# Down weights of a mixture-of-experts stage split in two counted halves, and a small copy moved from VectorE to ScalarE

## The reference

```
xe = zeros(E, CAP, d).at[se, pos].set(xf[tok])      # E = 64 experts, CAP = 256 slots each, d = 512
h  = silu(xe @ gate_proj) * (xe @ up_proj)          # 512 -> 192
ye = h @ down_proj                                  # 192 -> 512
out[tok] += ye[se, pos] * weight                    # added to the rows the tokens came from
```

## Time and profile before

| | |
|---|---|
| Median of three runs | 1779.56 us (1773.2 to 1784.63) |
| The profiled execution | 1779.15 us, with a span of 1777.3 us |
| Attention part | 0 to about 1183 us |
| Expert stage | about 1183 us to the end, about 594 us |
| Loads of one expert, time from issue to landing (median, whole run) | rows 4.6 us, gate/up 6.4 us, down 7.3 us |
| Bytes moved in the whole run | 311.91 MB |

### The profile page before, as it was taken

One profiled execution on the slowest core, in us unless ns is written; L12 is line 12 of the kernel. 1 busy time (PEld: TensorE's weight loads), 2 busy tenths in 40 slices (PEclk: granted clock), 3 DMA queues, 4 the chain that ended last, 5 costly groups with the idle time before them and its releaser, 6 DMA issues.

```text
span 1777.3 us, 25068 instructions
## 1 busy us (share of the span) xinstructions
PE 1576.7 (89%) x8112; PEld 1012.7 (57%) x8112; DVE 1211.1 (68%) x2706; ACT 982.4 (55%) x1922; POOL 956.0 (54%) x890
## 2 busy tenths in 40 slices
PE   5888899999999999999999989529999999999995
PEld 2444344544544444444444543229988888888884
DVE  3566587787787787787788776317876666665762
ACT  3345457656656656656665745215555555555552
POOL 4122243474464464464465456756676666665665
PEclk8889999999999999999999989759999999999997
DMA  9956743634544444343343240059999999999995
GB/s 333 293 166 205 222 137 109 190 129 153 171 143 152 143 145 135 116 123 114 101 114 96 57 109 23 25 184 252 258 241 253 256 262 252 255 262 256 244 253 84
DMA packets 148337, 311.91 MB, mean 175 GB/s; under 512 B 27674, under 2 KB 37786, under 8 KB 148208
## 3 DMA queue, kind: packets, MB, share of 16 engines
q1 hardware_dynamic: 109296, 238.89, 43.3%
q0 software_dynamic: 38912, 71.43, 18.1%
HBM read 141.25 MB, written 155.91 MB: 167 GB/s over the span
## 4 chain that ended last, share of the span: by engine, by line
PE 36%; DMA 22%; issue 10%; DVE 9%; POOL 5%; SPq 2%; ACT 1%; POOLq 0%; DVEq 0%; ACTq 0%
DMA out_rows<-y_slots,row_ids 18%; PE bank L686 6%; PE bank L698 5%; PE bank L677 4%; DMA q_stack<-x_t 2%; PE bank L616 2%; POOL slot_rows L1460 2%; PE bank L655 2%; SPq L440 2%; PE bank L720 2%; POOL out_rows L1509 1%; PE bank L609 1%; PE bank L642 1%; PE bank L595 1%; DVE row_stat L1073 1%
## 5 line engine op out<-in xcount | busy, mean ns | idle before, releaser
L1198 DVE TENSOR_REDUCE max_col<-bank 128x1 f32<-128x512 f32 x512 | 340.7, 684 | 148.5 <-PE bank L677 147.4
L953 ACT ACTIVATE p_t<-bank 128x512 f32<-128x512 f32 x512 | 297.9, 596 | 256.7 <-PE bank L686 252.0
L1448 POOL TENSOR_TENSOR p_sum<-p_t 128x512 f32<-128x512 f32 x128 | 162.1, 1282 | 330.6 <-ACT p_t L953 329.9
L1509 POOL DMA_INDIRECT out_rows<-y_slots,row_ids x128 | 221.8, 1733 | 197.4 <-DMA out_rows<-y_slots,row_ids 150.1
L1460 POOL DMA_INDIRECT slot_rows<-row,slot_i x256 | 268.1, 1047 | 78.2 <-issue 77.6
L686 PE MATMUL bank<-q_stack,k_stack 98*128 98x512 f32 x512 | 277.6, 543 | 15.1 <-DMA q_stack<-max_lo 14.5
L677 PE MATMUL bank<-k_stack,q_stack 96*128 96x512 f32 x512 | 213.4, 418 | 24.7 <-DVE max_col L1198 14.5
L686 PEld LDWEIGHTS bank<-q_stack,k_stack 98*128 98x128 f32 x512 | 98.5, 193 | 193.3 <-issue 176.1
L1499 POOL TENSOR_TENSOR down_lo<-down,down_hi 96x1024 fp32r<-96x1024 f32 x64 | 188.5, 2945 | 15.9 <-DVE down_hi L1356 15.9
L1325 DVE TENSOR_TENSOR x_slots_t_lo<-bank,x_slots_t_hi 128x512 fp32r<-128x512 f32 x128 | 88.3, 690 | 150.6 <-ACT x_slots_t_hi L1005 150.6
L795 PE MATMUL bank<-gate_up_hi,x_slots_t_hi 128*128 128x384 f32 x512 | 185.2, 362 | 0.6 <-DVE x_slots_t_lo L1325 0.5
(11 more groups left out here) (179 smaller groups left out, 3129.4 us busy)
## 6 DMA issues: line engine op xcount, KB each, us to landing
gate_up<-in_gate_up SPq DMA_DIRECT2D x64, 768.0 KB, 6.4
slot_rows<-row SPq DMA_DIRECT2D x64, 577.0 KB, 9.0
x_slots<-slot_rows SPq DMA_DIRECT2D x64, 577.0 KB, 4.6
k_stack<-prob SPq DMA_DIRECT2D x192, 128.0 KB, 2.9
down<-in_down SPq DMA_DIRECT2D x64, 384.0 KB, 7.3
q_stack<-x_t SPq DMA_DIRECT2D x128, 128.0 KB, 3.0
x<-in_x SPq DMA_DIRECT2D x16, 512.0 KB, 3.4
ctx<-in_ctx SPq DMA_DIRECT2D x16, 512.0 KB, 3.7
```

Source lines behind the costliest of these rows:

```text
L953: e.activation(p_t[step % 2][:, h, :], psum[n % 2][:, :], ACT.Exp, scale=SCALE).then_inc(free[n % 2], 1)
L1198: e.tensor_reduce(max_col[quad % 2][:, h, c:c + 1], psum[2 + n % 2][:, :], X, ALU.max, negate=True).then_inc(free[2 + n % 2], 1)
L1448: e.tensor_tensor(p_sum[:, h, :], p_t[(step - 1) % 2][:, h, :], p_t[step % 2][:, h, :], ALU.add).then_inc(p_sum_ok, 1)
L1509: e.indirect_dma_start(out=out, out_offset=bass.IndirectOffsetOnAxis(ap=row_ids[e_ % NI][:, q, :].bitcast(U32), axis=0), in_=ye[e_ % NY][: ...
```

## The change

POOL's subtraction for the low part of `down` is made in two pieces of 96x512, one for each half of the inner dimension, and each raises `dn_lo_ok` by one, so that an expert counts two. All waits on the count are restated: users of the weights and of the buffers wait for both halves. One wait is different in kind: SP's loop for expert k now waits for the first half of expert k + 3 only (`2 * (e_ + 4) - 1`). What it then loads into `down` is the buffer of expert k + 2, both halves of which were counted before.

`copy_ids` moves from VectorE's loop to ScalarE's, behind `down(t)` of the odd step and ahead of `split_gate_up`.

```
@@ sync
                 if k:
-                    w.wait_ge(dn_lo_ok, e_ - NB + 1)
+                    w.wait_ge(dn_lo_ok, 2 * (e_ - NB + 1))
                 e.dma_start(dn[i][:, :, :], a["down"][e_]).then_inc(weights_of[i], 16)
...
-                w.wait_ge(dn_lo_ok, min(e_ + 4, NEXP))
+                w.wait_ge(dn_lo_ok, min(2 * (e_ + 4) - 1, 2 * NEXP))
                 if e_ + NB < NEXP:
                     load_rows(e_ + NB)
@@ tensor, down(u)
-                w.wait_ge(dn_lo_ok, e_ + 1)
+                w.wait_ge(dn_lo_ok, 2 * (e_ + 1))
@@ scalar
+            def copy_ids(e_):
+                i = e_ % NB
+                w.wait_ge(rows_of[i], 16 * (e_ // NB + 1))
+                if e_ >= NI:
+                    w.wait_ge(added[(e_ - NI) % 2], 32 * ((e_ - NI) // 2 + 1))
+                e.copy(row_ids[e_ % NI][:, :, :], xe[i][:, :, T:T + 1].bitcast(I32)).then_inc(row_ids_ok, 1)
...
                 if t >= 0:
                     down(t)
+                if t % 2 and 0 <= t + 3 < U:
+                    copy_ids((t + 3) // 2)
@@ vector: copy_ids and its call are gone; in split_down
-                    w.wait_ge(dn_lo_ok, e_ - NW + 1)
+                    w.wait_ge(dn_lo_ok, 2 * (e_ - NW + 1))
@@ gpsimd, split_down
-                e.tensor_tensor(dn_lo[nw][:, :, :], dn[i][:, :, :], dn_hi[nw][:, :, :].bitcast(F32),
-                                ALU.subtract).then_inc(dn_lo_ok, 1)
+                for c in range(2):
+                    e.tensor_tensor(dn_lo[nw][:, c, :], dn[i][:, c, :], dn_hi[nw][:, c, :].bitcast(F32),
+                                    ALU.subtract).then_inc(dn_lo_ok, 1)
```

More of the change, by code:

```diff
@@ L1312, in _ @@
             w.wait_ge(slots_ok, B)
[L1314 to L1319, removed]
             def turn(u):
@@ L1364, in _ @@
                     turn_hidden(t + 1)
-                if t % 2 and 0 <= t + 3 < U:
-                    copy_ids((t + 3) // 2)
                 if t > -6 and (t + 5) // 2 < NEXP:
```

## The result

The changed kernel takes 1791.38 us (median of 11 runs, 1786.13 to 1797.12), the kernel before, run beside it, 1782.16 us (11 runs, 1773.2 to 1786.87). The ratio is **1.0044, 95% interval 1.0028 to 1.0060**: slower by 8 us. The forecast was 10 us less. The time lies in the range and within 1% of before, but on the wrong side of it. The profiled execution took 1791.63 us (span 1789.1, before 1777.3); as in the prediction, the working goes by the profiled pair, whose difference is 11.8 us.

What follows compares the result with a forecast made beforehand. The prediction took the adds' landing, stretched by loads on the shared DMA engines, as the bound. Earlier release gave -0.2 us x 52 = -10.4 us, all other parts 0: 1779.15 - 10.4 = 1768.7, stated as 1769 us, range 1752 to 1794.

Steps and rivals of the forecast that it cites:

- The bound: Expert stage: the landing of POOL's adds, stretched by loads sharing the DMA engines, sets the pace, 9.03 us a cycle.
- Earlier release: SP's loads in the expert stage go out 1.48 us earlier, into an underfilled DMA stretch: -0.2 us a cycle, -10.4 us.
- (a): Next cycle's adds: the load burst ends 1.48 us earlier, so they meet less of it, gaining 0.74 us a cycle.
- (b): The adds' last 1.48 us run beside the load burst and land 0.31 us later; ends 0 and 0.74.
- The unused share: DMA engines in the expert stage: 4% of time unused, 0.36 us a cycle, of which two thirds would be filled.
- TensorE's waits: TensorE's waits for rows, 22.3 us per 400, mostly go as rows come 1.48 us earlier; worth 0 us.
- Two subtractions for one: POOL's extra instruction and count are covered by its idle 2.35 and 4.35 us: 0 us.
- The copy: Row-number copy leaves VectorE for 0 us; on ScalarE, at 0.33 us each, also 0 us, ends 0 and +21.
- The casts: VectorE's cast of `down` lengthens POOL's add issues; moved up to 1.48 us, it hits as often: 0 us.
- the prediction's far end: VectorE's cast lies ahead of both POOL add issues and no longer lengthens them: -23 us.
- rival 3: Adds' tail beside the loads pays more than their head wins: slower, 1795 us, at most 1810; chance 0.18.
- rival 1: DMA engines are full and nothing moves: 1775 to 1783 us; chance 0.2.

Runs made afterwards that it cites:

- e8: Kernel before, gate/up not loaded from the sixth expert on except 64 bytes per partition: 1736.33 us against 1788.62, ratio 0.9698.
- e17: Kernel before with row-number copy on ScalarE and a 128x16 POOL memset ahead of the whole subtraction releasing SP: ratio 0.9934.
- e3: The change, but SP waits for both subtraction halves: 1782.37 us, ratio 1.0026 to the kernel before.
- e16: Kernel before with row-number copy on ScalarE, subtraction in halves, and a 128x16 POOL memset ahead of them releasing SP: ratio 0.9885.
- e2: Kernel before with only the copy of the row numbers moved to ScalarE: 1774.71 us, ratio 0.9992.
- e15: Kernel before with row-number copy on ScalarE and a 128x1154 POOL memset ahead of the whole subtraction releasing SP: ratio 1.0002.

## Why the prediction was wrong

**The bound** was right. The loop of the adds' landing sets the pace; 52 cycles give the difference of the spans, and e8 shows that the bytes of the loads stretch that landing (second landing 7.5 us instead of 8.25).

**Earlier release** is the step that failed. Its term (a) said that the burst ends 1.48 us earlier in the next cycle, so that the next adds meet less of it. Measured: the release came 1.1 us earlier, but the burst took 9.2 us to land, not 7.3, because it now ran beside the adds' tail. By the prediction's own sum it ends at 5.11 + 0.9 + 9.2 - 9.28 = +5.9 of the next cycle, where before it ended at 6.26 + 0.9 + 7.3 - 9.05 = +5.4. Later, not earlier; by its bytes it ends where it did (+4.6 and +4.4 in the table above). The first add accordingly lands where it did (6.38 against 6.47 us): (a) was worth 0.1 us, not 0.74. Term (b), 0.31 us, fits: the second landing is 0.23 us later, and the cycle with it, though no run has (b) without (a). With (a) near 0 and (b) at +0.2 to +0.3 the sum has the measured sign and size. Where the burst does end earlier, the head gains: in e17 it ends 1.2 us earlier and the first landing comes 0.9 us earlier, but the second, on which POOL waits, only 0.16. What misled me was to treat the burst as a block of fixed length that moves, when the same sharing by which I priced (b) also had to lengthen it. The Trainium skill ("DMA: Bandwidth & Descriptors", section "Queues, rings and completion order") lets each DMA engine take turns between the queues packet by packet; the longer landings agree with it, and by that rule both sides pay.

**The unused share**, from which I took two thirds, did not measure what could be won. The share rose from 0.96 to 0.97 and the GB/s fell from 255 to 248.

**TensorE's waits** did not go; they rose from 22.3 to 26.7 us, since rows issued 1.1 us earlier land 1.6 us later after issue. "1.48 us earlier they are there" rested on the same fixed length. That nothing hangs on them held: the results were 7 us old or more when POOL added them.

**Two subtractions for one** were put at 0 with POOL's idle time as cover. That cover hid nothing from SP, which waits for the end of the pair in e3: about 0.2% there. At +4, where the release does not depend on them, e16 shows no cost, within an interval of 0.8% width. In the change the first half takes 1.83 us and not 1.48, so SP is released 1.1 us earlier; that size was off too.

**The copy**: 0 for leaving VectorE and 0 on ScalarE, both right (e2, 0.9992), at 183 ns instead of the 331 taken as a bound.

**The casts**: 0 was right (the mean issue is 1723 ns), the reason given was not. The excess of the issue at 1398.62 is the end of `gate_up_lo`, not the cast; of the 23 us of excess the cast makes 3.4, so the -23 us of the prediction's far end could not have come from it.

**The rivals.** The outcome is nearest to rival 3 in mechanism, the tail paying more than the head wins, but at a size between it and rival 1, and its point of decision, an add delayed by over 0.74 us, was set too high: as the head won 0.1, 0.23 us sufficed. Its sign, a mean landing of over 6.4 us, appeared: 6.47 us from the second add's issue, 6.23 before.

**Open.** The head is freed at +4 because the burst ends earlier in the next cycle, and not at +4.9 because it ends where it did. Why a burst released at +4 is through in 5.3 us beside the adds and one released at +5 needs 6.0 to 6.2 is shown, not explained. Nor is it settled what makes the change 0.4% slower than e15 (1.0044 [1.0028, 1.0060] against 1.0002 [0.9982, 1.0022]), since they ran on different chips: the halves, against which e16 speaks, or the 0.2 us between them.

## What to carry to other kernels

When a burst of loads is moved beside other transfers, lengthen it by the same sharing that you charge to the others, and ask where it ends, not where it begins. A DMA share near 1 says nothing of throughput; read it together with the GB/s. The worth of a release is not linear in its time: here 1.15 to 1.3 us earlier gave nothing or cost 0.4%, 2.3 us gave about 1%, and 6.8 us cost 4.8%, so try several places, with a small instruction that carries the count, before splitting a large one.

## What was unexpected of the hardware

- Two 96x512 subtractions on POOL take 1.83 us each and overlap: 3.11 us for the pair against 2.96 for one 96x1024. A split for an early count gives 1.1 us here, not half of 2.96.
- A `tensor_tensor` of VectorE with both inputs in SBUF that is under way when POOL starts an indirect issue holds that issue until 1.4 us after its own end (2.38 instead of 1.55 us), in 31 issues of the kernel before; the cast of `down` does the same in 10. Cutting it in two pieces did not help (1725 ns in the mean against 1733), as the issue waits for both.
- In two 2 us stretches of the kernel after, around its loads at 1682.84 and 1691.02 (the answer to the earlier trace rows), shares near and over 1 go with very different rates:

```profile
1682.00:1684.00 2.00, 2.00 (x14) 1.71 (x12) 1.74 (x4) 0.82 (x3) 2.00 (x2) 1.00 0.99 132
1691.00:1693.00 2.00, 2.00 (x13) 1.84 (x12) 0.83 (x3) 0.59 (x2) 1.24 (x1) 1.00 1.12 243
```
